# Own rows' logit sums move from VectorE's reduction to ScalarE's accumulating output

## The chip, the cores and the metric

The kernel runs on one core of one Trainium2 chip. The metric is the device time of one execution in microseconds (us), less being better. Engines are called PE (TensorE, matrix products and transposes), DVE (VectorE), ACT (ScalarE), POOL (GpSimd, which here also issues the gathers by index and the accumulating copies) and SP (SyncE, which issues the other transfers).

## The reference

The program is two layers of graph attention (GATv2) over 20000 nodes of 512 features with 4 heads of 128, followed by a feed-forward part with merged weights. There are 10000 edges, sorted by destination, plus one loop per node. What the change touches is the attention of the edges:

```
xl = (x @ Wl + bl).reshape(N, H, C)
xr = (x @ Wr + br).reshape(N, H, C)
e = leaky_relu(xl[src] + xr[dst], 0.2)
logits = einsum('ehc,hc->eh', e, att)
m = segment_max(logits, dst); p = exp(logits - m[dst]); s = segment_sum(p, dst)
out = segment_sum(xl[src] * (p / s[dst])[..., None], dst)
```

The loop edge of a node has the same form with its own row in both places: its logit is leaky(xl[dst] + xr[dst]) times att, summed per head over 128 columns. The kernel calls this second half of the work "own".

## The kernel before, in words

Five stages follow each other, each a block in which all engines run: a first transform of all nodes, the edge pass of layer 0, a second transform, the edge pass of layer 1, and the feed-forward part with its merge of weights. The transforms write, for each node, two rows of 512 floats: its normed features and its product with Wl. The change is in `edge_pass` (from line 555), which runs twice.

An edge pass takes 80 tiles (T) of 128 edges; 5 tiles (G) form a group, over which the running maxima and sums of the softmax are made. Each engine has its own in-order program. It is written by `pipeline(n, steps)` (line 46): in iteration k each step (function, ahead) is done for tile k + ahead, in the order in which the steps stand. Waits between engines are on semaphores that count tiles; `need(engine, semaphore, value)` (line 54) waits only for a positive value.

One tile goes this way:

- POOL, `gather`: two transfers by index, of both rows of the destination nodes (into `nv`, L640) and of the source nodes' product (into `vs`, L642). It waits for `weighted`, t - 13, because the slots are a ring of 14 (R).
- PE, `transposes` (L874): four transposes of the destination features, once both transfers have landed. Then ACT, `copy_transposed` (L676): copy out of PSUM. It waits for `transposed` and for `root`, t - 1, that is, until the products of tile t - 2 are done, since `nT` has two slots.
- PE, `roots` (L882, L885): the product with Wr, eight matmul records, and the bias. PE's order is transposes of tile k + 6, then roots of tile k + 4.
- DVE, `pair_sums` (L734, L735), `leaky` over both halves (L740, 128x1024), `product` with att on the source half (L745). POOL multiplies the own half (`product_own`, L655).
- DVE, `logits` (L751): one reduction over both halves, 128x1024 to 128x8. Once in a group, `peaks` (L762 to L778), then `exps` on ACT (L683) and `sums_up` on DVE (L787 to L797).
- ACT, `weigh` (L691, L694): eight small products of the gathered rows with their shares, six tiles behind.
- POOL, `add_own` (L650): for every second tile, an accumulating transfer that adds the own halves of two tiles to the source halves. Then DVE, `accumulate` (L808, L813), nine tiles behind, and SP stores the result.

POOL's order in iteration k is product_own(k + 1), add_own(k - 7), gather(k + 7). ACT's is copy_transposed(k + 4), weigh(k - 6), exps(k). DVE's is leaky(k + 2), logits(k + 1), pair_sums(k + 3), product(k + 2), peaks(k + 1), sums_up(k), accumulate(k - 9), where peaks and sums_up do something for the last tile of a group alone.

Of the kernel before, what the change touches and what calls it, by code (L numbers as in the profile page):

```python
# [10 lines left out]
ALU = mybir.AluOpType  # L11
ACT = mybir.ActivationFunctionType
AX = mybir.AxisListType
# [3 lines left out]
H = 4  # L17
C = D // H
# [10 lines left out]
G = 5  # L29
# [8 lines left out]
ZR = 3  # L38
# [7 lines left out]
def pipeline(n, steps):  # L46

    for k in range(-max(a for _, a in steps), n):
        for step, ahead in steps:
            if 0 <= k + ahead < n:  # L50
                step(k + ahead)


def need(eng, sem, value):

    if value > 0:
        eng.wait_ge(sem, value)


def chunks(ap):  # L60
    return ap.rearrange("p (c n) -> p c n", c=KC)


def heads(ap):
    return ap.rearrange("p (h c) -> p h c", h=H)
# [14 lines left out]
def clear(nc, semaphores):  # L80
    with nc.Block() as block:  # L81
        @block.gpsimd
        def _(pool):
            for q in semaphores:
                pool.sem_clear(q)


def group(nc, c, name, products, **rings):

    s = {p: c.enter_context(nc.semaphore(f"{name}_{p}")) for p in products.split()}  # L90
    for p, n in rings.items():
        s[p] = [c.enter_context(nc.semaphore(f"{name}_{p}{u}")) for u in range(n)]
    c.callback(lambda: clear(nc, [q for v in s.values() for q in (v if type(v) is list else [v])]))
    return s
# [461 lines left out]
def edge_pass(nc, layer, g):  # L556
# [3 lines left out]
    T, w = g["T"], g["w"]  # L560
# [12 lines left out]
    with ExitStack() as c:  # L573
        def sb(name, shape, dt=F32):
            return c.enter_context(nc.sbuf_tensor(f"{name}_e{layer}", shape, dt))
# [3 lines left out]
        z = sb("z", [P, ZR, 2, D])  # L579
# [5 lines left out]
        lg = sb("lg", [P, 2, 2, H, G])  # L585
# [14 lines left out]
        best, gain, sums, scale4 = (sb(k, [P, H]) for k in ("best", "gain", "sums", "scale4"))  # L600
        first_row, joined = w1[:, 0, :], w1[:, 1, :]

        s = group(nc, c, f"e{layer}", "w_loaded w_high w_low b_loaded chain ready transposed featT root z leaky product product_own logit "
                  "bottom exps shares weighted summed trail_set trail_stored others_loaded "
                  "share_exps share_sums share_in share_T share_copied shared joined cleared",
                  stored=AR)
# [64 lines left out]
        @block.scalar  # L671
        def _(act):
            def copy_transposed(t):
                act.wait_ge(s["transposed"], t + 1)
                need(act, s["root"], t - 1)
                act.copy(nT[:, t % 2, :, :], chunks(psT[t % 2][:, :])).then_inc(s["featT"], 1)  # L676

            def exps(t):
                i, last = divmod(t, G)
                if last != G - 1:  # L680
                    return
                act.wait_ge(s["bottom"], i + 1)
                act.activation(ex[:, i % 2, :], ex[:, i % 2, :], ACT.Exp).then_inc(s["exps"], 1)  # L683

            def weigh(t):
                i, u, b = t // G, t % R, t % WR
                probs = ex[:, i % 2, 0:2 * H * G].rearrange("p (a h g) -> p a h g", a=2, h=H)
                act.wait_ge(s["shares"], i + 1)
                need(act, s["summed"], t - WR + 1)
                for h in range(H):  # L690
                    act.activation(w1[:, b, h * C:(h + 1) * C], vs[:, u, h * C:(h + 1) * C], ACT.Copy,  # L691
                                   scale=probs[:, 0, h, t % G:t % G + 1])
                for h in range(H):
                    last = act.activation(w2[:, b, h * C:(h + 1) * C], nv[:, u, 1, h * C:(h + 1) * C], ACT.Copy,  # L694
                                          scale=probs[:, 1, h, t % G:t % G + 1])
                last.then_inc(s["weighted"], 1)

            pipeline(T + G + 1, [(lambda t: copy_transposed(t) if t < T else None, 4),
                                 (lambda t: weigh(t - G - 1) if 0 <= t - G - 1 < T else None, 0),
                                 (lambda t: exps(t) if t < T else None, 0)])  # L700
            act.wait_ge(s["w_loaded"], 16)
            act.copy(whi[:, :, :], raw[:, :, :]).then_inc(s["w_high"], 1)
            act.wait_ge(s["share_in"], 1)
            act.activation(share[:, :, :], share[:, :, :], ACT.Exp).then_inc(s["share_exps"], 1)
            act.activation(gain[:, :], gain[:, :], ACT.Exp).then_inc(s["share_exps"], 1)
            act.wait_ge(s["share_T"], 1)
            act.copy(share_T[:, :, :], heads(psW[:, :])).then_inc(s["share_copied"], 1)

        @block.vector
        def _(dve):  # L710
            linked = 0

            def link(ins):
                nonlocal linked
                linked += 1
                ins.then_inc(s["chain"], 1)
                dve.wait_ge(s["chain"], linked)
# [11 lines left out]
            def pair_sums(t):  # L729
                u, b = t % R, t % ZR  # L730
                dve.wait_ge(got[u], got0[u] + 32 * (t // R + 1))
                dve.wait_ge(s["root"], t + 1)
                need(dve, s["logit"], t - ZR + 1)
                dve.tensor_tensor(z[:, b, 0, :], psR[t % 2][:, :], vs[:, u, :], ALU.add)  # L734
                dve.tensor_tensor(z[:, b, 1, :], psR[t % 2][:, :], nv[:, u, 1, :], ALU.add).then_inc(s["z"], 1)  # L735

# [10 lines left out]
            def logits(t):  # L747
                b, i = t % ZR, t // G
                dve.wait_ge(s["product"], t + 1)
                dve.wait_ge(s["product_own"], t + 1)  # L750
                dve.tensor_reduce(lg[:, i % 2, :, :, t % G], z[:, b, :, :].rearrange("p a (h c) -> p a h c", h=H), AX.X,  # L751
                                  ALU.add).then_inc(s["logit"], 1)

            def peaks(t):
                i, last = divmod(t, G)
                if last != G - 1:
                    return
                b, at = i % 2, i * G
                l, m, e = lg[:, b, :, :, :], peak[:, b, :, :], ex[:, b, :]
                factor = e[:, 2 * H * G:]  # L760
                dve.wait_ge(s["logit"], t + 1)
                link(dve.tensor_tensor(l[:, 1, :, :], l[:, 1, :, :], start_gap[:, at:at + G].unsqueeze(1).to_broadcast([P, H, G]),  # L762
                                       ALU.add))
                link(dve.tensor_tensor(m, l[:, 0, :, :], l[:, 1, :, :], ALU.max))
                if i:
                    link(dve.scalar_tensor_tensor(m[:, :, 0], top[:, i - 1, :, G - 1], gap[:, at:at + 1], m[:, :, 0],
                                                  ALU.add, ALU.max))
                link(dve.tensor_tensor_scan(flat(m), flat(gap4[:, i, :, :]), flat(m), -BIG, ALU.add, ALU.max))
                link(dve.tensor_tensor_scan(flat(top[:, i, :, :])[:, ::-1], flat(gap4_back[:, i, :, :])[:, ::-1], flat(m)[:, ::-1],
                                            -BIG, ALU.add, ALU.max))  # L770
                need(dve, s["weighted"], t - 2 * G + 1)
                dve.tensor_tensor(e[:, 0:2 * H * G].rearrange("p (a n) -> p a n", a=2), l.rearrange("p a h g -> p a (h g)"),
                                  flat(top[:, i, :, :]).unsqueeze(1).to_broadcast([P, 2, H * G]), ALU.subtract)
                if i:
                    dve.scalar_tensor_tensor(factor, top[:, i - 1, :, G - 1], gap[:, at:at + 1], top[:, i, :, 0],
                                             ALU.add, ALU.subtract).then_inc(s["bottom"], 1)
                else:
                    dve.memset(factor, -BIG).then_inc(s["bottom"], 1)  # L778
# [21 lines left out]
            def accumulate(t):  # L800
# [9 lines left out]
                else:  # L810
                    dve.wait_ge(s["summed"], t)
                    for h in range(H):
# [7 lines left out]
                               (lambda t: logits(t) if t < T else None, 1),  # L820
                               (lambda t: pair_sums(t) if t < T else None, 3),
                               (lambda t: product(t) if t < T else None, 2),
                               (lambda t: peaks(t) if t < T else None, 1),
                               (lambda t: sums_up(t - 1) if 1 <= t <= T else None, 1),
                               (lambda t: accumulate(t - lag) if t >= lag else None, 0)])

            dve.wait_ge(s["w_high"], 1)
# [29 lines left out]
            for h in range(H):  # L857
                last = dve.tensor_scalar(first_row[:, h * C:(h + 1) * C], first_row[:, h * C:(h + 1) * C], gain[:, h:h + 1], None,
                                         ALU.mult)
            link(last)  # L860
            dve.wait_ge(s["shared"], 1)
            for h in range(H):
                last = dve.scalar_tensor_tensor(joined[:, h * C:(h + 1) * C], psA[:, h * C:(h + 1) * C], scale4[:, h:h + 1],
                                                first_row[:, h * C:(h + 1) * C], ALU.mult, ALU.add)
# [35 lines left out]
def flat(ap):  # L900
    return ap.rearrange("p h g -> p (h g)")
# [621 lines left out]
```

## Time and profile before

| | us |
|---|---|
| Runs shown: median (lowest to highest of 3) | 3017.18 (3014.49 to 3019.19) |
| The profiled execution's own time | 3014.56 |
| Its span in the profile | 3012.7 |
| Busy in the span: PE / DVE / ACT / POOL | 2627.5 / 2505.0 / 1503.3 / 1236.6 |
| Stretch of the two edge passes, roughly | 535 to 1040 and 1585 to 2070 |

A row of the grouped view reads: line, engine, operation, output and input tiles, shapes, count, then busy time in us, mean ns of one, and the idle time of the engine just before, with what ended it. A row of the timeline reads: start in us, duration in us, engine, line, operation, tiles, and how many instructions were merged; in brackets the engine's idle time before it, with its releaser. PE's records are pipelined; "PEclk" is the clock that was granted, as a share of full speed.

### The profile page before, as it was taken

The page shows a single profiled execution, that of the slowest core. Times are in us where ns is not written, and L with a number is a line of the kernel's source. Part 1 is how long each engine was busy: PE and PEld are TensorE (multiplying, and loading weights), DVE is VectorE, ACT ScalarE, POOL GpSimd, SP SyncE. Part 2 cuts the span into 40 slices and gives each one's busy share as a digit, 9 for nine tenths or more (in the row PEclk, how much of TensorE's full clock was granted, in tenths as well). Part 3 has the DMA queues.
Part 4 walks back from the last instruction along what each step waited for, and adds up shares of the span by engine and source line. Part 5 has one row for each costly group of instructions (what it writes and reads, how often), then busy time and mean ns, then how long its engine had stood idle before and what let it go on. Part 6 is the DMA issues. An engine that isn't in the chain of part 4 may idle for free. (4 is left out here: it accounts for less than half of the span.)

```text
span 3012.7 us, 40248 instructions
## 1 busy us (share of the span) xinstructions
PE 2627.5 (87%) x11205; PEld 1801.0 (60%) x11205; DVE 2505.0 (83%) x5771; ACT 1503.3 (50%) x3651; POOL 1236.6 (41%) x1138
## 2 busy tenths in 40 slices
PE   6999999788888099999989888861899999969997
PEld 5777777333333078888864333330788888746665
DVE  7999998699999467777757999994988888379997
ACT  4545555155555333333323555553777788525554
POOL 0012220577776133333317777752333333014443
PEclk8999999899999599999999999985899999989998
DMA  9999999588887588888856888876999999469999
GB/s 326 340 308 319 320 323 342 179 235 243 231 238 211 142 272 279 269 265 266 263 197 204 243 239 237 237 186 202 385 357 352 347 349 344 140 183 250 249 250 160
DMA packets 321178, 789.66 MB, mean 262 GB/s; under 512 B 53838, under 2 KB 54384, under 8 KB 310746
## 3 DMA queue, kind: packets, MB, share of 16 engines
q1 hardware_dynamic: 220440, 540.20, 51.2%
q0 software_dynamic: 98064, 243.10, 33.3%
q10 hardware_dynamic: 2452, 3.79, 0.4%
q8 instruction: 92, 1.51, 0.2%
q14 instruction: 130, 1.06, 0.1%
HBM read 469.66 MB, written 329.28 MB: 265 GB/s over the span
## 5 line engine op out<-in xcount | busy, mean ns | idle before, releaser
L882 PE MATMUL bank<-wr,nT_e 128*128 128x512 f32 x1280 | 610.6, 622 | 0.5 <-DVE z_e L735 0.5
L1039 PE MATMUL bank<-whi,t_hi 128*128 128x512 f32 x1256 | 524.0, 417 | 23.7 <-DVE t_lo L406 23.7
L1041 PE MATMUL bank<-whi,t_lo 128*128 128x512 f32 x1256 | 498.1, 397 | 0.0
L1040 PE MATMUL bank<-wlo,t_hi 128*128 128x512 f32 x1256 | 497.7, 396 | 0.0
L882 PEld LDWEIGHTS bank<-wr,nT_e 128*128 128x128 f32 x1280 | 244.3, 201 | 253.1 <-issue 252.4
L906 POOL DMA_INDIRECT vin<-touched,node_slot x157 | 173.5, 1105 | 333.2 <-DMA vin<-rows 329.8
L906 POOL DMA_INDIRECT g_vin<-touched,node_slot x157 | 176.9, 1127 | 323.2 <-DMA g_xin<-in_x 289.8
L676 ACT COPY nT_e<-bank 128x512 f32<-128x512 f32 x160 | 93.6, 585 | 409.3 <-PE bank L885 354.9
L1039 PEld LDWEIGHTS bank<-whi,t_hi 128*128 128x128 f32 x1256 | 237.2, 189 | 73.7 <-issue 17.2
L1041 PEld LDWEIGHTS bank<-whi,t_lo 128*128 128x128 f32 x1256 | 237.2, 189 | 58.8
L655 POOL TENSOR_TENSOR z_e<-z_e,v_att 128x512 f32<-128x512 f32 x160 | 204.8, 1280 | 158.6 <-DVE z_e L740 157.8
L640 POOL DMA_INDIRECT nv_e<-rows,dst_row x160 | 200.2, 1252 | 166.6 <-POOLq L81 130.6
L1231 PE MATMUL bank<-g_hi,whi 128*128 128x512 f32 (+1 forms) x640 | 264.8, 414 | 0.0
L1040 PEld LDWEIGHTS bank<-wlo,t_hi 128*128 128x128 f32 x1256 | 237.8, 189 | 44.8
L1398 POOL DMA_DIRECT2D out<-f_y x157 | 135.7, 868 | 293.7 <-DVE f_y L1434 293.6
L978 ACT CAST t_hi<-bank 128x512 fp32r<-128x512 f32 (+1 forms) x157 | 91.6, 584 | 329.3 <-PE bank L1041 329.1
L1232 PE MATMUL bank<-g_hi,wlo 128*128 128x512 f32 (+1 forms) x640 | 251.5, 393 | 0.0
L1233 PE MATMUL bank<-g_lo,whi 128*128 128x512 f32 (+1 forms) x640 | 251.1, 392 | 0.0
L1007 DVE TENSOR_TENSOR t_lo<-bank,t_hi 128x512 fp32r<-128x512 f32 (+1 forms) x157 | 108.2, 689 | 153.0 <-PE bank L1041 153.0
L874 PE MATMUL bank<-ident,nv_e 128*128 128x128 f32 x640 | 111.5, 300 | 134.7 <-DMA vs_e<-rows,src_row 134.3
L296 POOL DMA_INDIRECT ordered<-pair,place x79 | 76.8, 973 | 350.4 <-DVE place L458 350.4
L691 ACT ACTIVATE w_e<-vs_e,ex_e 128x128 f32<-128x128 f32 x640 | 204.1, 392 | 12.7 <-DVE acc_e L808 6.6
(247 smaller groups left out, 6001.5 us busy)
## 6 DMA issues: line engine op xcount, KB each, us to landing
rows<-t_row SPq DMA_DIRECT2D x312, 512.0 KB, 4.4
w_e<-w_e POOLq DMA_DIRECT2D x80, 512.0 KB, 4.7
touched<-acc_e SPq DMA_DIRECT2D x160, 256.0 KB, 4.3
xin<-in_x SPq DMA_DIRECT2D x156, 256.0 KB, 4.7
xTin<-in_xT SPq DMA_DIRECT2D x156, 256.0 KB
vin<-rows SPq DMA_DIRECT2D x156, 256.0 KB, 4.0
g_vin<-rows SPq DMA_DIRECT2D x156, 256.0 KB
g_xin<-in_x SPq DMA_DIRECT2D x156, 256.0 KB
```

The source lines that it names most:

```text
L640: pool.indirect_dma_start(nv[:, u, :, :].rearrange("p a d -> p (a d)"), None, whole, bass.IndirectOffsetOnAxis(g["dst_row"][:, t:t + 1].bi ...
L655: pool.tensor_tensor(z[:, b, 1, :], z[:, b, 1, :], att[:, :], ALU.mult).then_inc(s["product_own"], 1)
L691: act.activation(w1[:, b, h * C:(h + 1) * C], vs[:, u, h * C:(h + 1) * C], ACT.Copy, scale=probs[:, 0, h, t % G:t % G + 1])
L882: pe.matmul(psR[b][:, :], nT[:, b, cc, :], wr[:, cc, :], start=(cc == 0), stop=False)
L906: pool.indirect_dma_start(to, None, g["touched"][layer][:, :], bass.IndirectOffsetOnAxis(g["node_slot"][0:r, t:t + 1].bitcast(U32), 0), bo ...
L1039: pe.matmul(ps, hi[:, cc, :], whi[:, cc, :], start=(cc == 0), stop=False)
L1040: pe.matmul(ps, hi[:, cc, :], wlo[:, cc, :], start=False, stop=False)
L1041: last = pe.matmul(ps, lo[:, cc, :], whi[:, cc, :], start=False, stop=(cc == KC - 1))
L1231: pe.matmul(psG[cc][:, 0:n], whi[:, k, cols], hi[:, b, k, 0:n], start=(k == 0), stop=False)
L1232: pe.matmul(psG[cc][:, 0:n], wlo[:, k, cols], hi[:, b, k, 0:n], start=False, stop=False)
L1233: last = pe.matmul(psG[cc][:, 0:n], whi[:, k, cols], lo[:, b, k, 0:n], start=False, stop=(k == KC - 1))
L1398: pool.dma_start(out[t * P:t * P + r, :], y[0:r, u, :], accum_op=ALU.add).then_inc(added[u], 16)
```

## The change

The own half of the product is no longer summed by DVE. ACT sums it, one head at a time: a Copy of 128x128 in place, whose accumulator output goes to one column of `lg`. ACT gets a new step `own_logits`, placed between the copy and the weighing, and the copy's lead goes from 4 to 5. DVE's reduction takes 128x512 in the place of 128x1024 and no longer waits for POOL's product. The maxima and sums of a group (`peaks`, `sums_up`) come one iteration later on DVE, and `peaks` and `pair_sums` wait for a new semaphore, `own_logit`.

```diff
+            def own_logits(t):
+                i, b = t // G, t % ZR
+                act.wait_ge(s["product_own"], t + 1)
+                need(act, s["bottom"], i - 1)
+                for h in range(H):
+                    last = act.activation(z[:, b, 1, h * C:(h + 1) * C], z[:, b, 1, h * C:(h + 1) * C], ACT.Copy,
+                                          accum_out=lg[:, i % 2, 1, h, t % G:t % G + 1])
+                last.then_inc(s["own_logit"], 1)
+
...
-            pipeline(T + G + 1, [(lambda t: copy_transposed(t) if t < T else None, 4),
+            pipeline(T + G + 1, [(lambda t: copy_transposed(t) if t < T else None, 5),
+                                 (lambda t: own_logits(t) if t < T else None, 1),
                                  (lambda t: weigh(t - G - 1) if 0 <= t - G - 1 < T else None, 0),
                                  (lambda t: exps(t) if t < T else None, 0)])
...
                 need(dve, s["logit"], t - ZR + 1)
+                need(dve, s["own_logit"], t - ZR + 1)
                 dve.tensor_tensor(z[:, b, 0, :], psR[t % 2][:, :], vs[:, u, :], ALU.add)
...
             def logits(t):
                 b, i = t % ZR, t // G
                 dve.wait_ge(s["product"], t + 1)
-                dve.wait_ge(s["product_own"], t + 1)
-                dve.tensor_reduce(lg[:, i % 2, :, :, t % G], z[:, b, :, :].rearrange("p a (h c) -> p a h c", h=H), AX.X,
-                                  ALU.add).then_inc(s["logit"], 1)
+                dve.tensor_reduce(lg[:, i % 2, 0, :, t % G], heads(z[:, b, 0, :]), AX.X, ALU.add).then_inc(s["logit"], 1)
...
                 dve.wait_ge(s["logit"], t + 1)
+                dve.wait_ge(s["own_logit"], t + 1)
...
                                (lambda t: product(t) if t < T else None, 2),
-                               (lambda t: peaks(t) if t < T else None, 1),
-                               (lambda t: sums_up(t - 1) if 1 <= t <= T else None, 1),
+                               (lambda t: peaks(t) if t < T else None, 0),
+                               (lambda t: sums_up(t - 1) if 1 <= t <= T else None, 0),
                                (lambda t: accumulate(t - lag) if t >= lag else None, 0)])
```

## Rows read from the trace of the kernel before

**Rows 1.** Windows of each pass: busy us and count by engine, PEclk, DMA share, GB/s.
```profile
621.00:990.00 369.00, 307.25 (x838) 136.72 (x837) 356.58 (x636) 200.96 (x621) 270.26 (x225) 0.95 0.83 228
1650.00:2015.00 365.00, 315.95 (x863) 141.45 (x863) 355.08 (x639) 197.80 (x611) 272.55 (x226) 0.95 0.85 233
```

**Rows 2.** Groups by line, whole span: DVE's operations on both halves and on one.
```profile
L740 DVE SCALAR_TENSOR_TENSOR z_e<-z_e 128x1024 f32<-128x1024 f32 x160 | 194.5, 1216 | 0.1
L751 DVE TENSOR_REDUCE lg_e<-z_e 128x8 f32<-128x1024 f32 x160 | 193.8, 1211 | 0.0
L735 DVE TENSOR_TENSOR z_e<-bank,nv_e 128x512 f32<-128x512 f32 x160 | 108.5, 678 | 0.0
```

**Rows 3.** Timeline: the reductions of tiles 14 and 19.
```profile
632.58 1.21 DVE L751 TENSOR_REDUCE lg_e<-z_e 128x8 f32<-128x1024 f32 x1
659.55 1.21 DVE L751 TENSOR_REDUCE lg_e<-z_e 128x8 f32<-128x1024 f32 x1
```

**Rows 4.** Timeline: from one accumulating transfer to the weighing behind its gather, tile 27.
```profile
668.27 0.95 POOL L650 DMA_DIRECT2D w_e<-w_e  x1
669.52 1.31 POOL L640 DMA_INDIRECT nv_e<-rows,dst_row  x1 [0.30 <-ACT w_e L694]
671.14 0.97 POOL L642 DMA_INDIRECT vs_e<-rows,src_row  x1 [0.30 <-issue]
677.10 0.66 PE L874 MATMUL bank<-ident,nv_e 128*128 128x128 f32 x4 [1.95 <-DMA vs_e<-rows,src_row]
681.12 0.50 PE L885 MATMUL bank<-root_bias_e,bias_ones 33*128 33x512 f32 x1
681.71 0.58 ACT L676 COPY nT_e<-bank 128x512 f32<-128x512 f32 x1 [3.55 <-PE bank L885]
683.37 1.27 ACT L694 ACTIVATE w_e<-nv_e,ex_e 128x128 f32<-128x128 f32 x4
```

**Rows 5.** Timeline: the same for tile 33, where PE's clock fell.
```profile
702.00 0.96 POOL L650 DMA_DIRECT2D w_e<-w_e  x1
710.63 1.00 PE L874 MATMUL bank<-ident,nv_e 128*128 128x128 f32 x4 [3.24 <-DMA vs_e<-rows,src_row]
716.34 0.49 PE L885 MATMUL bank<-root_bias_e,bias_ones 33*128 33x512 f32 x1
718.59 1.26 ACT L694 ACTIVATE w_e<-nv_e,ex_e 128x128 f32<-128x128 f32 x4
723.42 0.98 POOL L650 DMA_DIRECT2D w_e<-w_e  x1
```

**Rows 6.** Timeline: gathers with no accumulating transfer ahead (tile 2; tile 28).
```profile
546.54 0.95 POOL L642 DMA_INDIRECT vs_e<-rows,src_row  x1 [0.30 <-issue]
551.70 1.11 PE L874 MATMUL bank<-ident,nv_e 128*128 128x128 f32 x4 [0.83 <-DMA vs_e<-rows,src_row]
...
675.18 0.98 POOL L640 DMA_INDIRECT nv_e<-rows,dst_row  x1 [0.16 <-issue]
676.46 0.96 POOL L642 DMA_INDIRECT vs_e<-rows,src_row  x1 [0.30 <-issue]
```

**Rows 7.** Timeline: PE's bias products of tiles 14 and 77, both passes.
```profile
620.67 0.49 PE L885 MATMUL bank<-root_bias_e,bias_ones 33*128 33x512 f32 x1
972.10 0.50 PE L885 MATMUL bank<-root_bias_e,bias_ones 33*128 33x512 f32 x1
...
1658.87 0.49 PE L885 MATMUL bank<-root_bias_e,bias_ones 33*128 33x512 f32 x1
2007.80 0.50 PE L885 MATMUL bank<-root_bias_e,bias_ones 33*128 33x512 f32 x1
```

**Rows 8.** ACT's one accumulating operation so far, by line: min/median/max ns.
```profile
L1157 ACT ACTIVATE g_units<-bank,g_unit_bias x160: 287/688/742, 2129.0 to 2633.2; 128x512 f32<-128x512 f32 x156, 128x32 f32<-128x32 f32 x4
L1157 ACT ACTIVATION_READ_ACCUMULATOR g_units<-bank,g_unit_bias x160: 185/206/262, 2129.6 to 2633.4; 128x1 f32 x160
```

**Rows 9.** Timeline: ACT's last exponentials of the second pass.
```profile
2030.88 0.24 ACT L683 ACTIVATE ex_e<-ex_e 128x44 f32<-128x44 f32 x1 [3.84 <-DVE ex_e L775]
```

More of the change, by code:

```diff
@@ L601, in edge_pass @@
         first_row, joined = w1[:, 0, :], w1[:, 1, :]
-        s = group(nc, c, f"e{layer}", "w_loaded w_high w_low b_loaded chain ready transposed featT root z leaky product product_own logit "
+        s = group(nc, c, f"e{layer}", "w_loaded w_high w_low b_loaded chain ready transposed featT root z leaky product product_own own_logit logit "
                   "bottom exps shares weighted summed trail_set trail_stored others_loaded "
```

## The prediction

> **What bounds the kernel now.** I read the page's slices first, to find the two edge passes, then a window over the steady part of each, then the timeline around single tiles. The windows show DVE busy for 356.6 of 369 us and 355.1 of 365 us (97%), PE for 307 and 316, POOL for 270 and 273, ACT for only 201 and 198 [rows 1]. By shares the passes belong to DVE. The reader should then look at what a tile waits for. DVE alone needs 26.97 us for five tiles (659.55 - 632.58) where it does not stand still [rows 3], 5.39 us a tile. The true pace comes from PE's bias products: 63 tiles from tile 14 to tile 77 take 351.43 us in the first pass and 348.93 in the second [rows 7], 350.2 on average, 5.56 a tile. So there is about 0.17 us a tile in which DVE, too, waits; it waits for PE, and PE's transposes wait for the gathers ("DMA vs_e", 1.95 and 3.24 us [rows 4, 5]). DVE is first by a small margin only, and behind it stands a chain POOL, transfer, PE, ACT that shares of busy time don't show.
>
> **What goes from DVE.** The reduction of 128x1024 takes 1211 ns. An elementwise operation on 128x1024 takes 1216 and one on 128x512 678 [rows 2], so half the reduction should take about 675 ns: 0.53 us less, 160 times, 85 us of DVE work in all. DVE alone would then need 26.97 - 5 x 0.53 = 24.3 us for five tiles, 4.86 a tile. Were nothing else in the way, 63 x (5.56 - 4.86) = 44 us a pass and 88 us in all would go.
>
> **What comes to ACT.** Four pairs a tile of an accumulating Copy of 128x128 and a read of the accumulator. The only accumulating operation of the trace takes 688 ns for 512 columns and 287 for 32, so 0.835 ns a column, and its read 206 ns [rows 8]. The Copy of 512 columns takes 0.58 us [rows 4]; less 384 columns that is 0.26. From rows 4, copy start to the end of eight weighings is 684.64 - 681.71 = 2.93 us, far under the sum of nine durations: neighbours overlap by about 0.1. I take 0.16 for the Copy and 0.19 for the read, 1.4 us for four pairs. The lower end is 1.0 (reads overlapped by half), the upper 4 x (0.26 + 0.206) = 1.9 (no overlap at all). ACT's work for a tile rises from some 2.9 to 4.3 us, still below any pace in question: by its load ACT is no bound.
>
> The page "ScalarE: Activation LUTs" of the Trainium skill (section "What ACT_TABLE_LOAD costs") gives 186 ns plus 0.833 ns a column for an operation with immediate scale and bias, and an overlap of about 93 ns. The slope agrees with the 0.835 worked out above; by its fixed part a Copy of 128 columns would take 200 ns of ACT instead of my 160, which makes 0.14 us a tile more in the chain below and, by an estimate, 6 us more in the end. It has no price for the read.
>
> **What is moved, and the chain that it closes.** Two edits look like bookkeeping: the copy's lead goes from 4 to 5, and own_logits stands ahead of weigh. Before, ACT did weigh(m - 10) right behind the copy of tile m; after, it does copy(m), own_logits(m - 4), weigh(m - 11). Now follow POOL: gather(m + 3) waits until tile m - 11 is weighed (a ring of 14), and where there is an add_own it waits, ahead of the gather, for the same tile. And copy(m) waits for the roots of tile m - 2, which PE does right behind the transposes of tile m, which wait for gather(m). So after the change each gather is released by the one three tiles earlier; before, weigh(m - 10) released gather(m + 4), four tiles. One turn of this chain, from the rows of tile 27, with an accumulating transfer in it [rows 4]: add_own to first gather 1.25, to second gather 1.62, to transposes 5.96, to the end of the bias product 4.52, to the copy 0.09, to the end of the weighing 2.93: 16.37 us. Without the accumulating transfer, which is every second tile: first to second gather 1.28 [rows 6]; landing 5.16 for an early gather in a quiet queue and no more than 5.96, of which I take 5.5 [rows 4, 6]; then 4.52 + 0.09 + 2.93 as above: 14.3.
>
> Before: the mean of both, 15.35, over four tiles is 3.8 us a tile, well under 5.56. The trace shows this slack: the weighing of tile 23 ends at 719.85 and the add_own that wants it starts at 723.42 [rows 5]. After: plus 1.4 for the own sums and 0.1 for POOL to wake, 17.9 and 15.8, mean 16.85, over three tiles: 5.62 us a tile. A second turn, over four tiles, goes from gather through two transposes and two roots (one more at 4.5): 16.37 + 4.5 + 1.4 + 0.1 = 22.4, or 5.59 a tile. Both lie above DVE's 4.86, and just above the pace of today. So DVE's saving turns into waiting, and the new bound is slightly slower than the old one.
>
> **PE's clock.** In rows 5 PE had waited 3.24 us for the gather; from transposes to the end of the bias product it then took 716.83 - 710.63 = 6.20 us, in place of the 4.52 of tile 27, which followed a wait of 1.95. Granted clock in the windows is 0.95 [rows 1], so such falls (from 2.4 to 1.2 GHz) are occasional today. After the change the chain waits on these landings all the time, and each fall of 1.7 us stands inside the chain itself, with no DVE work beside it. I take one fall in three turns: 1.7 / 3 / 3 = 0.19 us a tile. Bounds: none, and one each turn, 0.57.
>
> **The sum.** 5.62 + 0.19 = 5.81 us a tile; 63 tiles make 366.0 against 350.2, 15.8 us more a pass. The first 14 tiles are paced by PE, ahead of the chain, in both kernels: nothing. The end of a pass: after the roots of tile 77 ACT has a copy, five own sums and six weighings before its last exponentials, 0.5 + 5 x 1.4 + 6 x 2.44 = 22.1 us; today that instruction starts 2030.88 - 2008.30 = 22.6 us after them [rows 7, 9], held by DVE: nothing. The later peaks and sums_up ride on the same shift and are covered by the wait of DVE. New waits on own_logit at pair_sums: own_logits(m - 4) ends 2 us after the roots of tile m - 2, and the pair sums that want it need roots a tile later, 4.5 us; no cost. If that cover fails it is 1 us a tile at most. Two passes: +31.6 us on the profiled execution's 3014.56, 3046; the median of the runs shown lies 2.6 above that execution, so 3048.
>
> **Rivals.**
> 1. *The chain closes but the clock holds.* At 5.62 a tile the passes take 7.6 us more together: 3025. With the cheap ends (own sums 1.0, all landings 0.3 sooner) the turn is 16.1 and the tile 5.38, 23 us less in all: 2994. For it: tile 27's wait of 1.95 us cost no clock, and turns of equal length spread the waits. Against: waits today are uneven.
> 2. *DVE stays the bound and the saving comes through* (the other side). Place: the steady part of both passes; price: down to 4.86 us a tile, 88 us less, 2929. It decides if a turn of the chain stays under 3 x 4.86 = 14.6 us, that is, if landings with ACT's part shorten by over 2 us. By the Trainium skill's "Perfetto Trace Analysis" (section "Identifying the Most-Contended Engine") the engine of highest occupancy is the one to relieve, which is DVE here and speaks for this case. Windows speak for it, too; against it stands that no row has a landing under 5.16. In part (5.2 a tile, if ACT runs further ahead than I see) it would be 2972.
> 3. *ACT's sums are dear.* Reads without overlap (1.9) and a fall of the clock each turn: 16.85 + 0.5 + 1.7 = 19.05, 6.35 a tile, 100 us more: 3117.
>
> **Chances.** Forecast 0.50, rival 1 0.20, rival 2 in full or part 0.20, rival 3 0.10. The range 2985 to 3095 holds the forecast, nearly all of rival 1 and the near half of rival 3; it leaves out most of rival 2. A measurement of this kernel can tell about 0.2% (6 us) from no change. Faster by more: rival 2 and a small part of 1, 0.23. Within: a part of rival 1 and the forecast's low edge, 0.10. Slower: 0.67.
>
> **What would show it.** Right: the reduction at about 675 ns; DVE's busy share in the windows falls from 97% to 83 to 88%; POOL's add_own (L650) or its first gather waits for ACT's weighing on most even iterations, where it now does so only at a pass's end; PE's idle time ahead of the transposes grows, PEclk falls below 0.95; reductions in the steady part 5.6 to 6 us apart. Wrong: if DVE stays above 95% busy and reductions come 4.2 us apart within a group, rival 2; if ACT never idles for PE, rival 3. If four pairs of ACT take under 0.8 us, or L650 shows no wait, my chain is mis-sized.

## The result, and the profile after

The changed kernel takes 3087.06 us (median of 4 runs, 3081.82 to 3088.45), against 3017.87 before: a ratio of 1.0228, 95% interval 1.021 to 1.0246. That is 69 us more; the forecast was 3048, 31 more. The sign and the place were right, and the size forecast was less than half of the measured one.

First the windows over the steady part of both passes, which answer to [rows 1]: busy us by engine (PE, PE's loads, DVE, ACT, POOL), then PEclk, DMA share, GB/s.

```profile
621.00:1015.00 394.00, 322.94 (x853) 143.31 (x851) 378.25 (x645) 279.32 (x1166) 271.93 (x226) 0.92 0.77 216
1660.00:2050.00 390.00, 322.14 (x849) 143.94 (x848) 366.56 (x622) 268.26 (x1120) 279.50 (x227) 0.92 0.76 214
```

DVE is still busy for 96 and 94% of them. Someone who stops here would say that DVE is the bound and has more to do. The groups of 650 to 950, in the same kernel, say where that busy time comes from (answers to [rows 2, 8]):

```profile
L756 DVE TENSOR_TENSOR z_e<-z_e,v_att 128x512 f32<-128x512 f32 x51 | 70.3, 1379 | 0.0
L683 ACT ACTIVATE z_e<-z_e 128x128 f32<-128x128 f32 x204 | 60.4, 301 | 0.0
L683 ACT ACTIVATION_READ_ACCUMULATOR z_e<-z_e 128x1 f32 x204 | 38.8, 190 | 0.0
L761 DVE TENSOR_REDUCE lg_e<-z_e 128x4 f32<-128x512 f32 x51 | 34.6, 678 | 0.0
```

The halved reduction takes 678 ns, as forecast (675). But DVE's product on the source half, 689 ns in the same stretch before, is now 1379 ns on average: the saving seems to be spent on an instruction that was not touched. The longest lasts 2.37 us. Two of them, one of the usual length and one long, with POOL's products on the other half beside them:

```profile
746.87 1.27 POOL L655 TENSOR_TENSOR z_e<-z_e,v_att 128x512 f32<-128x512 f32 x1 [1.36 <-DVE z_e L751]
748.50 0.68 DVE L756 TENSOR_TENSOR z_e<-z_e,v_att 128x512 f32<-128x512 f32 x1
...
758.54 2.25 DVE L756 TENSOR_TENSOR z_e<-z_e,v_att 128x512 f32<-128x512 f32 x1
758.95 1.28 POOL L655 TENSOR_TENSOR z_e<-z_e,v_att 128x512 f32<-128x512 f32 x1
```

The first begins when POOL's product is over (748.14) and takes 0.68 us. The second has POOL's product beside it and ends 0.56 us behind it (760.79 against 760.23). All 63 products of DVE in the trace that last over 1 us end so, 0.55 to 0.56 us behind one of POOL's. The waits of the same stretch, by waiter and releaser (us in total, times, longest), tell the other half:

```profile
ACT nT_e L676 <- PE bank L895: 74.1, 43, 4.9
...
PE bank L884 <- DMA vs_e<-rows,src_row: 51.6, 29, 3.6
...
POOL nv_e L640 <- ACT w_e L703: 32.3, 20, 3.6
POOL w_e L650 <- ACT w_e L703: 19.4, 19, 2.4
```

POOL waits for ACT's weighing ahead of 39 of some 51 tiles; before, there were four such waits of 0.3 us in this stretch. One turn of that chain in the timeline, which answers to [rows 4]:

```profile
748.08 0.97 POOL L650 DMA_DIRECT2D w_e<-w_e  x1
749.35 2.54 POOL L640 DMA_INDIRECT nv_e<-rows,dst_row  x1 [0.30 <-issue]
752.19 0.97 POOL L642 DMA_INDIRECT vs_e<-rows,src_row  x1 [0.30 <-issue]
757.70 0.66 PE L884 MATMUL bank<-ident,nv_e 128*128 128x128 f32 x4 [1.00 <-DMA vs_e<-rows,src_row]
761.72 0.50 PE L895 MATMUL bank<-root_bias_e,bias_ones 33*128 33x512 f32 x1
762.31 0.59 ACT L676 COPY nT_e<-bank 128x512 f32<-128x512 f32 x1 [1.43 <-PE bank L895]
765.14 1.26 ACT L703 ACTIVATE w_e<-nv_e,ex_e 128x128 f32<-128x128 f32 x4
766.67 0.97 POOL L640 DMA_INDIRECT nv_e<-rows,dst_row  x1 [0.60 <-ACT w_e L703]
```

From the second row on, each row is released by the one above it or stands behind it in an engine's queue, and the last row is the same instruction as the second, three tiles on: 766.67 - 749.35 = 17.3 us, 5.8 a tile. The pace of the passes comes from PE's bias products of tiles 14 and 77, as in [rows 7]:

```profile
625.96 0.49 PE L895 MATMUL bank<-root_bias_e,bias_ones 33*128 33x512 f32 x1
998.22 0.50 PE L895 MATMUL bank<-root_bias_e,bias_ones 33*128 33x512 f32 x1
...
1695.57 0.49 PE L895 MATMUL bank<-root_bias_e,bias_ones 33*128 33x512 f32 x1
2077.96 0.50 PE L895 MATMUL bank<-root_bias_e,bias_ones 33*128 33x512 f32 x1
```

63 tiles in 372.26 and 382.39 us, 5.99 a tile against 5.56.

### The profile page after: what moved, and what is told of

It is laid out like the page before. It is cut to its first block and busy times, and to the rows that moved or that the text cites. A ratio compares the mean times of both kernels' runs of the same rounds, so it can differ in the third digit from the quotient of the medians.

```text
span 3085.0 us, 41696 instructions
## 1 busy us (share of the span) xinstructions
PE 2657.7 (86%) x11205; PEld 1812.7 (59%) x11205; DVE 2535.2 (82%) x5771; ACT 1687.3 (55%) x4931; POOL 1239.4 (40%) x1138
## 5 line engine op out<-in xcount | busy, mean ns | idle before, releaser
L892 PE MATMUL bank<-wr,nT_e 128*128 128x512 f32 x1280 | 635.4, 644 | 0.0
L892 PEld LDWEIGHTS bank<-wr,nT_e 128*128 128x128 f32 x1280 | 253.7, 209 | 268.3 <-issue 268.3
L640 POOL DMA_INDIRECT nv_e<-rows,dst_row x160 | 206.7, 1292 | 255.5 <-POOLq L81 130.5
L916 POOL DMA_INDIRECT vin<-touched,node_slot x157 | 170.0, 1083 | 339.2 <-DMA vin<-rows 327.7
L339 ACT CAST t_hi<-xTin 128x512 fp32r<-128x512 f32 (+1 forms) x157 | 97.1, 618 | 204.0 <-PE bank L1051 203.9
```

What stands on the lines that cost most here:

```text
L640: pool.indirect_dma_start(nv[:, u, :, :].rearrange("p a d -> p (a d)"), None, whole, bass.IndirectOffsetOnAxis(g["dst_row"][:, t:t + 1].bi ...
L892: pe.matmul(psR[b][:, :], nT[:, b, cc, :], wr[:, cc, :], start=(cc == 0), stop=False)
L916: pool.indirect_dma_start(to, None, g["touched"][layer][:, :], bass.IndirectOffsetOnAxis(g["node_slot"][0:r, t:t + 1].bitcast(U32), 0), bo ...
```

## The experiments

Two theories stood against each other. CHAIN: the ring of gathers is closed over three tiles through ACT. PORT: DVE's product is held up when POOL's product runs at the same time (a meeting), and DVE is the bound. The steady parts are the 63 tiles from tile 14 to tile 77 of both passes, 126 in all, measured at PE's bias products. All times are medians; ratios are to the kernel before, with the 95% interval.

**1. att from PSUM (DVE's product taken out of the meetings).**

```diff
+    psAtt = banks[6]
...
+            link(dve.tensor_copy(psAtt[:, :], att[:, :]))
...
-                dve.tensor_tensor(z[:, b, 0, :], z[:, b, 0, :], att[:, :], ALU.mult).then_inc(s["product"], 1)
+                dve.tensor_tensor(z[:, b, 0, :], z[:, b, 0, :], psAtt[:, :], ALU.mult).then_inc(s["product"], 1)
```

> The changed kernel, with one thing different: DVE's product on the source half reads att from a spare PSUM bank, copied there once a pass, so the product has one operand in SBUF and not two. Two theories of the 69 us. CHAIN (that of the prediction): gather, transposes, roots, copy, own sums, weighing, next gather but two is closed at 5.6 to 5.9 us a tile, and DVE only waits on it; then this changes little, 3070 to 3087. PORT: in the trace after, DVE's product lasts up to 2.3 us where POOL's product_own runs at the same time (mean 1.38 us over 650 to 950, against 0.69 before), so DVE is still the bound, at a price that it pays to POOL; then the product returns to 0.68 us, DVE loses 0.7 to 0.8 us a tile over some 126 tiles, and the time falls by 80 to 100 us, to 2990 to 3005.

Measured 3067.97 (1.0169, 1.0152 to 1.0186), 19 us under the changed kernel. (The trace is that of its slowest execution, 3075.69.) DVE's product and its `accumulate` in the same stretch:

```profile
L758 DVE TENSOR_TENSOR z_e<-z_e,bank 128x512 f32<-128x512 f32 x51 | 34.4, 674 | 0.0
L820 DVE SCALAR_TENSOR_TENSOR acc_e<-acc_e,same,w_e 128x512 f32<-128x512 f32 x41 | 45.7, 1115 | 0.0
```

1379 ns became 674: the long products were the meeting with POOL's. But the meetings did not all go. `accumulate`, whose product also reads two operands from SBUF, took a part of them over: 1115 ns on average, against 741 in the changed kernel (L818 there, 40 times, 29.7 us), and some small operations of `peaks` and `sums_up` did so too. So the 0.7 us a tile saved in the product, some 89 us over 126 tiles, did not leave DVE: over the two windows used above its busy time fell from 744.8 to 723.3 us. PORT is real, and the 19 us are what one instruction's share in it costs, not its whole price. They lie between both expectations, closer to CHAIN; that PORT is not the main bound rests on experiments 2, 4 and 7.

**2. The weighing one tile sooner (the chain opened to four tiles).**

```diff
-            pipeline(T + G + 1, [(lambda t: copy_transposed(t) if t < T else None, 5),
-                                 (lambda t: own_logits(t) if t < T else None, 1),
+            pipeline(T + G + 1, [(lambda t: copy_transposed(t) if t < T else None, 4),
+                                 (lambda t: own_logits(t) if t < T else None, 0),
```

> The changed kernel, with ACT's copy leading by 4 and its own sums by 0 (after: 5 and 1). Copy and own sums keep their distance to each other; only the weighing comes one tile sooner behind them, as it did before the change, so that a gather is released by the one four tiles earlier and not three. CHAIN: one turn of 16.9 us over four tiles is 4.2 a tile, no bound any more, DVE's saving comes through: 2930 to 2980. PORT: DVE's product still meets POOL's product_own; 3060 to 3090. If both bounds stand side by side: a small part, 3040 to 3070.

Measured 3027.57 (1.0041, 1.0028 to 1.0054): 60 us back, between the ranges of the two theories and in neither. Most of the loss is the chain's; but DVE's saving did not come through as CHAIN wanted. Here ACT's exponentials wait 59.1 us in 300 (650 to 950) for DVE's peaks, against 13.4 in the changed kernel.

**3. Both edits.**

> Both edits: att read from PSUM by DVE's product, and the weighing one tile sooner. CHAIN and PORT both give DVE alone as the bound here, 4.9 to 5.1 us a tile, 2930 to 2960. If the two bounds stand side by side, then only this one gets there and each edit alone falls short of it. If this does not come under 3000, a third cause is at work.

Measured 3020.17 (1.0004, 0.9988 to 1.002), 7 us under experiment 2. Not under 3000: a third cause. In its trace ACT's exponentials wait 61.6 us in 300 for DVE's peaks, against 10.9 in the kernel before, with the next tile's copy for PE queued behind them; and PE still waits for gathers.

**4. The own sums behind the weighing.**

```diff
-                                 (lambda t: own_logits(t) if t < T else None, 1),
                                  (lambda t: weigh(t - G - 1) if 0 <= t - G - 1 < T else None, 0),
+                                 (lambda t: own_logits(t) if t < T else None, 1),
```

> The changed kernel, with ACT's own sums placed behind the weighing instead of ahead of it; leads unchanged (5 and 1). The gathers still hang on the one three tiles earlier, but the turn is shorter by the own sums, which the trace after shows at 1.2 us (four pairs, 742.96 to 744.15). CHAIN: 1.2 us off a turn over three tiles is 0.4 us a tile, 50 us in all: 3035 to 3045. PORT: same as the changed kernel, 3080 to 3090, or a few us either way as POOL's product shifts.

Measured 3033.01 (1.0059, 1.0042 to 1.0076): 54 us less for an exchange of two lines, against 50 expected by CHAIN and nothing by PORT. DVE's product is still long here (1180 ns in the same stretch).

**5. The lead alone, on the kernel before** (`copy_transposed` 4 to 5, nothing else).

> The kernel before, with the copy's lead alone raised from 4 to 5: the gathers then hang on the one three tiles earlier, with no own sums on ACT. CHAIN: the mean turn of 15.4 us over three tiles is 5.15 a tile, under the 5.56 of today, so the lead by itself costs little: 3018 to 3035, and half or more of the 69 us needs the own sums on top. If the lead by itself is worth more than 40 us, the turn is longer than the rows of before say.

Measured 3041.88 (1.0082, 1.0065 to 1.0099): 23 us for one digit, 7 above the range expected. The turn of 15.4 us over three tiles is below the mean pace, yet it costs. A part of the 23 us may be PORT's: DVE's product takes 807 ns here over 650 to 950, against 689 before. What each has in it was not separated.

**6. DVE's reduction work put back.**

```diff
-                dve.tensor_reduce(lg[:, i % 2, 0, :, t % G], heads(z[:, b, 0, :]), AX.X, ALU.add).then_inc(s["logit"], 1)
+                dve.tensor_reduce(lg[:, i % 2, 0, :, t % G], heads(z[:, b, 0, :]), AX.X, ALU.add)
+                dve.tensor_reduce(twice[:, t % 2, :], heads(z[:, b, 0, :]), AX.X, ALU.add).then_inc(s["logit"], 1)
```

> The changed kernel, with DVE doing its halved reduction twice, the second into a spare tile that nobody reads: DVE has the reduction work of before again, and all else is as after the change. CHAIN: DVE's 0.6 us a tile falls into its waiting: 3087 to 3110. PORT or DVE itself as the bound of the changed kernel: the work adds in full, 126 to 160 tiles of 0.6, 3165 to 3185; if the extra work spares DVE's product the meetings with POOL's (1.38 back to 0.7), it comes out even, and DVE's product shows it.

Measured 3087.49 (1.0231, 1.0214 to 1.0249), the same as the changed kernel to 0.5 us. What the change takes from DVE is worth nothing in it. Most of the added work was paid back by fewer meetings: DVE's product was 1083 ns here over 650 to 950, and over the two windows DVE's busy time rose from 744.8 to 762.6 us, although some 88 us of reductions were added. The rest fell into waiting. Both theories had room for this outcome (CHAIN, and PORT with fewer meetings), so it does not decide between them.

**7. Double own sums** (four more accumulating copies on ACT, of att into spare banks).

```diff
+        again, spare = sb("again", [P, 2, H]), banks[6:8]
...
+                need(act, s["own_logit"], t - 1)
+                for h in range(H):
+                    act.activation(spare[t % 2][:, h * C:(h + 1) * C], att[:, h * C:(h + 1) * C], ACT.Copy,
+                                   accum_out=again[:, t % 2, h:h + 1])
```

> The changed kernel, with four more accumulating copies on ACT ahead of the own sums (128 columns of att each, into a spare bank, their sums unused). CHAIN: 1.2 us more in a turn over three tiles is 0.4 a tile, 50 us more: 3130 to 3145 (ACT's load, 5.5 us a tile, is then near the pace, so it may be 10 more). PORT or DVE as the bound: ACT's load stays off the path, 3087 to 3100.

Measured 3153.43 (1.0441, 1.0415 to 1.0467), 66 us above the changed kernel: 1.2 us more of ACT in each turn cost 0.5 a tile in the steady parts (817.9 against 754.7 us), above CHAIN's 3130 to 3145 and within the 10 us that it allowed for ACT's load, and far from PORT's figure. ACT is busy for 81% of a steady stretch (292.58 of 359 us, from 621 on) and DVE for 86% (307.58): neither is full, and the turn is what got longer. The count of falls of PE's clock, explained in experiment 8, also rises, from 33 to 41.

**8. A filler on PE** (the changed kernel; one unused product behind each tile's roots).

```diff
+            def filler(t):
+                pe.matmul(banks[7][:, :], ident[:, :], wr[:, 0, :], start=True, stop=True)
+
-            pipeline(T, [(transposes, 6), (roots, 4)])
+            pipeline(T, [(transposes, 6), (roots, 4), (filler, 4)])
```

> The changed kernel, with one more product of 128x128 by 128x512 on PE behind the roots of each tile, into a spare bank that nobody reads: 0.86 us of PE a tile, in the place of idle time before the transposes (1.08 us a tile on average). CLOCK: the falls (33 in the steady part, 1.77 us each, in the chain) come from PE's waits of 2 to 3.6 us; shorter waits make most of them go, up to 45 us less, while PE's own work delays the turns in which it did not wait by up to 0.86: net 3050 to 3080. If falls only go along and cost nothing: the filler adds to the chain where PE did not wait, 3095 to 3130.

Measured 3074.84 (1.0186, 1.0169 to 1.0203): 12 us less with 0.86 us more work on PE in every tile. Its window over the first pass (columns as above):

```profile
621.00:1015.00 394.00, 370.53 (x1007) 158.97 (x1005) 382.31 (x658) 285.16 (x1189) 276.58 (x232) 0.99 0.79 221
```

The granted clock is 0.99 against 0.92. A fall of the clock shows in the timeline as a bias product that begins late after the transposes ahead of it: 4.02 us without a fall, and over 4.4 us is counted as one. In the 126 steady tiles the falls go from 33 to 1, and the steady parts get 30 us shorter (754.7 to 724.8). Some 16 of these are lost again elsewhere, 9 of them by tile 14 of the first pass, which PE now reaches at 635.19 and not at 625.96.

**9. The gather first** (POOL's `gather` ahead of `product_own`), on experiment 3 and on the kernel before.

> The kernel with att in PSUM and the weighing one tile sooner (3020 us), with POOL's gather moved ahead of its product in each iteration. In that kernel DVE's pair sums still wait up to 4.1 us for PE, PE for the gather, and the gather stands behind POOL's product, which waits for DVE's leaky: a second chain (LOOP) over four tiles on which the reduction doesn't lie. With the gather first it turns over five tiles. If LOOP is what still holds it: 2940 to 2985. If it is the load of the transfers or POOL: 3010 to 3025.

> The kernel before, with POOL's gather alone moved ahead of its product. LOOP holds DVE there by 0.17 us a tile (5.56 against 5.39), so this gives 10 to 25 us: 2993 to 3008. If it gives nothing, DVE's small waits in the kernel before have another source.

Measured 3029.28 (1.0043, 1.0027 to 1.006) and 3019.28 (1.0003, 0.9994 to 1.0013). A miss twice: the loop through POOL's product, which I had named as the third cause, is not what holds either kernel's total. In the second, though, the steady parts are 8 us shorter than before (692.5 against 700.4 us) and the rest of the span is 13 longer, so that the loop may hold a part of the steady pace; what the new order costs outside it was not followed up. What the first of them waits for instead stands in its waits, 650 to 950:

```profile
ACT ex_e L693 <- DVE ex_e L787: 70.5, 10, 7.3
POOL nv_e L641 <- ACT w_e L704: 64.6, 16, 5.9
...
PE bank L886 <- ACT nT_e L677: 33.6, 10, 3.9
```

ACT stands at the exponentials of a group until DVE has its peaks, which the change moved one iteration later; behind it stand the copy that PE wants and the weighing that the gather wants.

**10. Exponentials one iteration later**, with the gather first and with it last.

```diff
-                                 (lambda t: exps(t) if t < T else None, 0)])
+                                 (lambda t: exps(t - 1) if 1 <= t <= T else None, 0)])
```

> The kernel with att in PSUM, the weighing one tile sooner and the gather first (3029 us), with ACT's exponentials of a group one iteration later. In that kernel PE waited 33.6 us in 300 for ACT's copy, which stood behind the exponentials, and those waited up to 7.3 us for DVE's peaks, late since the change. If this HEAD-OF-LINE wait is what held it, nothing but DVE is left: 4.9 to 5.2 us a tile, 2935 to 2975. If not, 3015 to 3030.

> The same with POOL's gather last, as in both kernels: att in PSUM, weighing one tile sooner, exponentials one iteration later (3020 us without that). The LOOP over leaky, POOL's product, gather, PE and pair sums is still four tiles long. If it holds: 3005 to 3020. If the exponentials alone did the harm: 2940 to 2980, like the one beside it.

Measured 3015.76 (0.9997, 0.9987 to 1.0006) with the gather first, and 2986.78 (0.9905, 0.9886 to 0.9924) with it last. The second is 33 us under experiment 3 and faster than both kernels. It lies above its 2940 to 2980, and I had expected the other order to be the better one; with the gather first, the total falls in the 3015 to 3030 of "if not", and the waits show POOL's product late for ACT (24.1 us in 300, 4.1 without this edit). The window of the fast one:

```profile
621.00:970.00 349.00, 297.40 (x842) 132.82 (x840) 332.71 (x650) 277.39 (x1170) 264.61 (x225) 0.97 0.87 245
```

**11. The price of the meetings, chains open:** the last two kernels with att from SBUF, and the kernel before with att from PSUM.

> Weighing one tile sooner, gather first, exponentials later, but DVE's product with att from SBUF as in both kernels. Against the one with att in PSUM it prices PORT alone once the chains are open: DVE's product meets POOL's, 0.4 to 0.7 us a tile, 50 to 90 us more than e12, 2990 to 3040. If it equals e12, the meetings of the two engines have no price.

> The kernel of 2987 us (weighing one tile sooner, exponentials later, att in PSUM), with att from SBUF again. PORT: DVE's product meets POOL's, as in the others: 1.1 us mean in place of 0.67, 0.45 us a tile, some of it in DVE's remaining waits: 3005 to 3035. If it is equal to 2987, the meetings cost nothing and the order on ACT did it all.

> The kernel before, with att in PSUM for DVE's product. There the product takes 0.69 us on average against 0.68 alone, since the full reduction and the pair sums lie beside POOL's product: PORT has nothing to give, 3012 to 3020.

Measured 3051.62 (1.0114, 1.0096 to 1.0132), above the range, though only 36 above its pair (50 to 90 were expected); 3012.59 (0.998, 0.997 to 0.9989), 26 above its pair, with DVE's product at 1042 ns over 650 to 950; and 3013.70 (0.9982, 0.9972 to 0.9991), 4 under the kernel before. The last two came as expected. Opening the chain and moving the exponentials, without att in PSUM, turns the change into a gain of 5 us (3012.59 against 3017.80 for the kernel before, run beside it).

## Why the prediction was half right

**Right.** The bound read from the rows: gathers that hang on the weighing, three tiles apart. Experiments 2 and 4 take it apart and give 60 and 54 us back; 7 lengthens it and costs 66; 6 shows that DVE's saving is worth nothing, since putting the work back costs nothing. The reduction came at 678 ns. POOL's waits for ACT, PE's longer waits for the gathers (51.6 us against 42.9 over 650 to 950) and a granted clock under 0.95 came where they were forecast. The own sums cost 1.19 us (four pairs, 757.27 to 758.46), not 1.4:

```profile
757.27 0.31 ACT L683 ACTIVATE z_e<-z_e 128x128 f32<-128x128 f32 x1
757.49 0.19 ACT L683 ACTIVATION_READ_ACCUMULATOR z_e<-z_e 128x1 f32 x1
...
758.46 1.26 ACT L700 ACTIVATE w_e<-vs_e,ex_e 128x128 f32<-128x128 f32 x4
```

The prediction has one slip in its sums, on which the forecast does not rest: four copies of 200 ns in place of 160 are 0.16 us more, not 0.14.

**Wrong: the step "PE's clock".** I took one fall in three turns, 14 in 126 tiles, at 1.7 us. The size of one was right: 58.2 us for 33 falls, 1.77 each. Their number was more than twice as high, four in five turns. The count was there to be had: by the same measure the trace before already has 20 falls in its 126 steady tiles (34 us), and I had looked at one. All 33 stand behind idle times of PE of 1.7 to 4.0 us, waits for a gather; the granted clock then fell from 2.4 to 1.2 GHz for a part of the tile. The length of the wait alone does not tell: four waits of 1.8 to 2.6 us in the same tiles have no fall behind them. If each fall stands in the chain in full, the steady tile without them took (754.65 - 58.2) / 126 = 5.53 us, a little under my 5.62. In the terms of the sum that is falls 58 in place of 24 (+34) and the turn itself -12, together the 23 us by which the steady parts (+54) exceed the forecast's 31.6. Experiment 8 confirms at least half of it by intervention: the falls gone, the steady parts are 30 us shorter, even with PE's extra work in them; the full 58 is arithmetic. The page "TensorE: Matmul & The Clock Gate" of the Trainium skill (section "Why this matters for your kernels") warns of throughput drops after idle gaps between bursts of matmuls. The traces agree, and show falls behind gaps as short as 1.7 us.

**Wrong: the step "the first 14 tiles: nothing".** Tile 14 came 5.3 us later in the first pass (625.96 against 620.67) and 5.2 us later after the start of the second. Experiment 2, which opens the chain to four tiles, reaches it at 621.48, and experiment 4, which leaves it at three, at 626.03: the ring binds as soon as ACT weighs. Of the 72.3 us between the spans, 54.3 lie in the steady parts and 18 outside them, for which I had nothing; the remaining 7.5 come behind tile 77, 5.4 after the first pass and 2.1 after the second. There ACT's last exponentials start 22.8 and 23.1 us after PE's last steady bias product, near my 22.1; but before the change they start 20.4 us after it in the first pass, and I had read only the second (22.6). The other 5 us are open.

**Not seen: the meeting of DVE's and POOL's products.** It is in none of my terms. The full reduction and the pair sums, which read one operand from SBUF, used to lie beside POOL's product, and keep their length there (1211 and 679 ns). With the reduction halved and POOL late, DVE's product, with two operands in SBUF, meets it and waits. Taking this one instruction out of the meetings gives 19 us (experiment 1), while others of DVE come into them; what all of them cost in this kernel was not isolated. With the chain open the same edit is worth 7 us (2 against 3), and with the exponentials moved as well 26 and 36 (experiment 11). "SBUF — State Buffer" of the Trainium skill (section "SBUF: two separate sides") states such a lock between a DVE operation with two SBUF inputs and a GpSimd operation that reads SBUF, taken by whichever starts first. The traces agree on the lock: 1379 against 674 ns for the same product. On the order they do not bear the page out: by the recorded starts DVE's product is the earlier one in 48 of the 63 long cases (758.54 against 758.95 in the rows above), and it is DVE's that waits in all of them. When each took its ports the records do not say. The meetings also spoil the sign that I had named: I expected DVE's busy share to fall to 83 to 88%, and it stayed at 94 to 96% while DVE was not what held the kernel.

**Rival 2**, DVE as the bound and 2929 us, was not near in any order tried: the best, experiment 10, is at 5.2 us a tile, with three changes on top. Its last 0.3 us over DVE's 4.86 are, by its trace, mostly DVE still standing idle (5% of the window, some 0.25 us a tile), and meetings of `accumulate` (870 ns on average over 650 to 950, in place of 741).

## What to carry to other kernels

Before an operation moves to a half idle engine, write down what that engine's in-order queue releases and how many tiles later the ring comes round; a digit of lead in a list of steps can be worth more than the operation (23 us here with no work moved at all). An engine's busy share counts the time in which an instruction is held by another engine, so compare the mean duration of untouched instructions before it is called the bound. And when one instruction has been freed, look whether another has taken its place. And where PE waits for transfers, price the fall of its clock by its frequency in the new regime, not in the old one.

## What the hardware showed that I had not expected

- DVE's product of 128x512 with two SBUF operands lasts up to 2.37 us in place of 0.68 while POOL runs an elementwise product, and ends 0.56 us behind it. Reading one operand from PSUM frees it (674 ns, experiment 1) at no cost of its own (676 ns in the kernel before with that edit); but DVE's next instruction with two SBUF operands can then be the one that is held (`accumulate`, 1115 ns in place of 741).
- Useless work can pay: 0.86 us of PE a tile raised the granted clock from 0.92 to 0.99 and made the kernel 12 us faster.
- An accumulating Copy of 128x128 and its read follow each other at 0.30 us a pair (four from 757.27 to the next instruction at 758.46), although they last 0.30 and 0.19 us.
